# First edge loop of a four-layer graph network: the order of its turned one-hots, and the order of the work that prepares it

## The reference

```python
past, future = (edge_index[0], edge_index[1])
x_past = x[past]
x_future = x[future]
fwd_in = jnp.concatenate([x_future, x_past, edge_attr], axis=1)
flow_fwd = _mlp(fwd_in, W1f, b1f, W2f, b2f)
fwd_agg = jax.ops.segment_sum(flow_fwd, future, num_segments=x.shape[0])
bwd_in = jnp.concatenate([x_past, x_future, edge_attr], axis=1)
flow_bwd = _mlp(bwd_in, W1b, b1b, W2b, b2b)
bwd_agg = jax.ops.segment_sum(flow_bwd, past, num_segments=x.shape[0])
```

## Time and profile before

| | us |
|---|---|
| median of 3 runs | 2804.22 (2803.76 to 2804.41) |
| the profiled execution | 2801.62 |
| its span | 2799.8 |
| first table matmul starts (L893) | 819.76 |
| first and last `hidden` start (L926) | 862.4 and 1646.3 |

### The profile page before, as it was taken

One profiled execution on the slowest core, in us unless ns is written; L12 is line 12 of the kernel. 1 busy time (PEld: TensorE's weight loads), 2 busy tenths in 40 slices (PEclk: granted clock), 3 DMA queues, 4 the chain that ended last, 5 costly groups with the idle time before them and its releaser, 6 DMA issues. The chain is left out here.

```text
span 2799.8 us, 70675 instructions
## 1 busy us (share of the span) xinstructions
PE 2212.1 (79%) x26560; PEld 1628.7 (58%) x26560; DVE 1636.7 (58%) x4376; ACT 1368.2 (49%) x3156; POOL 1532.0 (55%) x1701
## 2 busy tenths in 40 slices
PE   0428787788727999999999967999999859995895
PEld 0103333333316888888888854666666559995773
DVE  5825444444405666666666656999999835552001
ACT  1005333333316888887888856888888600000110
POOL 2007777777756777777777734888888700000000
PEclk9967666656558999999999987999999969998997
DMA  8874444444330433343333425777777340007856
GB/s 352 363 288 112 113 113 114 113 114 113 109 89 16 163 120 118 118 157 125 117 118 118 163 102 153 199 192 200 199 192 200 94 83 3 3 3 313 334 228 288
DMA packets 252686, 427.70 MB, mean 153 GB/s; under 512 B 128564, under 2 KB 214222, under 8 KB 242725
## 3 DMA queue, kind: packets, MB, share of 16 engines
q1 hardware_dynamic: 194630, 337.86, 34.0%
q0 software_dynamic: 54800, 83.75, 12.3%
q10 hardware_dynamic: 2924, 1.57, 0.2%
HBM read 233.42 MB, written 209.72 MB: 158 GB/s over the span
## 5 line engine op out<-in xcount | busy, mean ns | idle before, releaser
L331 POOL DMA_INDIRECT sorted_edges<-s_records,s_index x400 | 476.3, 1191 | 311.5 <-issue 307.9
L803 POOL TENSOR_TENSOR e_ohw<-e_oh,e_rec 128x512 bf16<-128x512 bf16 x314 | 474.3, 1530 | 4.9 <-DVE e_oh L1056 4.9
L1524 PE MATMUL m_p_acc<-m_prod,m_oh 128*128 128x344 f32 x1250 | 400.6, 464 | 33.4 <-DVE m_prod L1585 22.6
L1524 PEld LDWEIGHTS m_p_acc<-m_prod,m_oh 128*128 128x128 f32 x1250 | 226.2, 191 | 148.1 <-issue 56.2
L1566 DVE TENSOR_TENSOR m_prod<-m_rec,m_coef 128x256 f32<-128x256 f32 x471 | 233.3, 546 | 0.0
L809 POOL TENSOR_TENSOR e_part<-e_rest,e_part 128x256 bf16<-128x256 f32 x157 | 104.0, 662 | 226.6 <-ACT e_part L871 226.6
L859 ACT ACTIVATE e_ohw<-e_oh,e_rec 128x128 bf16<-128x128 bf16 x628 | 216.2, 394 | 0.0
L1056 DVE TENSOR_TENSOR e_oh<-e_iota,e_rec 128x1024 bf16<-128x1024 f32 x157 | 212.2, 1353 | 0.2 <-DVE e_w_parts L91 0.2
L1782 PE MATMUL q_p_next<-q_g,pair 128*128 128x96 bf16 x4725 | 202.3, 207 | 0.0
L1782 PEld LDWEIGHTS q_p_next<-q_g,pair 128*128 128x128 bf16 x4725 | 201.3, 98 | 0.0
L1073 DVE COPY e_strip<-e_p_aw 128x512 f32<-128x512 f32 (+1 forms) x325 | 200.6, 660 | 0.0
(11 more groups left out here) (347 smaller groups left out, 4904.3 us busy)
## 6 DMA issues: line engine op xcount, KB each, us to landing
dense_strips<-e_strip SPq DMA_DIRECT2D x25, 3200.0 KB, 10.0
pair<-dense_strips SPq DMA_DIRECT2D x49, 1600.0 KB, 19.0
m_rec<-sorted_edges SPq DMA_DIRECT2D x138, 526.0 KB, 3.9
sorted_edges<-s_neg SPq DMA_DIRECT2D x5, 12560.0 KB, 68.5
pair<-dense_strips POOLq DMA_DIRECT2D x25, 800.0 KB, 8.9
e_rec<-sorted_edges SPq DMA_DIRECT2D x156, 108.0 KB, 2.3
sorted_edges<-s_records,s_index POOLq DMA_INDIRECT x400, 3.9
m_rec<-sorted_edges SPq DMA_DIRECT2D x12, 394.5 KB, 3.9
```

The lines of the kernel that those rows point to most:

```text
L331: pool.indirect_dma_start(dram["edges"], bass.IndirectOffsetOnAxis(ap=index[u % RING][:, c:c + 1], axis=0), record[u % RING][:, c, :], Non ...
L803: i = g_.tensor_tensor(ohw[g % 4][:, :, k, :], oh[s][:, :, 0, :], rec[s][:, :, c:c + 1].to_broadcast([P, G, P]), ALU.mult)
L1524: i = mm(p_acc[d % 2][:, 0:TERMS], oh[g % 4][:, t % G, :], prod[g % 3][:, t % G, :], start=(t % NB == 0), stop=(t % NB == NB - 1), skip_gr ...
```

## The change

1. In the loop, PE's `turn` is split into `turn_one_hots` and `turn_records`, both for group j+5, one-hots first. ACT's `copy_oh` stands ahead of `copy_rec`. SP's next load into a buffer of records waits for `rec_turned` in place of `turned`.
2. The 18 loads behind `d_b` are issued by SP, between the second and the third load of records, and no longer by ACT.
3. On DVE the fills and the `identb` cast stand ahead of the tables; `cut_weights`, with its wait for `d_b`, stands behind the fourth cut (i = 3); `one_hots(0)` to `one_hots(5)` follow the last six cuts, one each, and the loop makes only the later ones.

```diff
@@ sync @@
-                turned.before(sp, g, U)
+                rec_turned.before(sp, g, U)
...
             for g in range(2):
                 load(g)
+            sp.wait_ge(setup, 1)
+            for k, (wn, name) in enumerate(((1, "f"), (0, "b"))):
+                for i in range(6):
+                    sp.dma_start(w1e[16 * i:16 * i + 16, k, :], io["L0_gnn_W1" + name][2 * D:2 * D + 16, :]).then_inc(d_b, 16)
+                sp.dma_start(b1[k * H1:(k + 1) * H1, :], io["L0_gnn_b1" + name].unsqueeze(1)).then_inc(d_b, 16)
+                sp.dma_start(w2[k * H1:(k + 1) * H1, wn, :], io["L0_gnn_W2" + name]).then_inc(d_b, 16)
+                sp.dma_start(b2[:, :, wn, :], io["L0_gnn_b2" + name].unsqueeze(0).unsqueeze(0).to_broadcast([P, G, D])).then_inc(d_b, 16)
             for g in range(2, U):
                 load(g)
@@ scalar @@
-            act.wait_ge(setup, 1)
-            for k, (wn, name) in enumerate(((1, "f"), (0, "b"))):
-                for i in range(6):
-                    act.dma_start(w1e[16 * i:16 * i + 16, k, :], io["L0_gnn_W1" + name][2 * D:2 * D + 16, :]).then_inc(d_b, 16)
...
-                staged(j, (middle, 2), (copy_rec, 5), (copy_oh, 5), (weigh_first, 4), (relu1, 4), (weigh_last, 4), (relu2, 3))
+                staged(j, (middle, 2), (copy_oh, 5), (copy_rec, 5), (weigh_first, 4), (relu1, 4), (weigh_last, 4), (relu2, 3))
@@ tensor @@
-            def turn(g):
+            def turn_one_hots(g):
+                s = g % U
+                onehots.after(pe, g)
+                ohT_copied.before(pe, g, 1)
+                pe.sem_inc(prime, 1)
+                for k in range(2):
+                    for t in range(G):
+                        i = nc.tensor.transpose(p_oh[:, k, t, :], oh[s][:, t, k, :], identb[:, :])
+                turned.set_by(i)
+
+            def turn_records(g):
...
-                staged(j, (turn, 5), (hidden, 4), (second, 3), (sums, 1), (dense, 2))
+                staged(j, (turn_one_hots, 5), (turn_records, 5), (hidden, 4), (second, 3), (sums, 1), (dense, 2))
@@ vector @@
+            for i in range(TABLES):
+                n, to, y = table(i)
+                tab_hi.after(dve, i)
+                tab_low.before(dve, i, 2)
+                dve.sem_inc(prime, 1)
+                tab_cut.set_by(V.tensor_tensor(tab_rest[i % 2][:, 0:n, :], y, to[:, :, 0, :], ALU.subtract))
+                if i == 3:
+                    dve.wait_ge(d_b, 288)
+                    cut_weights(dve, V, w_chain, w1e[:, :, :].rearrange("p k h -> p (k h)"), w1_parts)
+                if i >= TABLES - READY:
+                    one_hots(i - (TABLES - READY))
+
+            def later_one_hots(g):
+                if g >= READY:
+                    one_hots(g)
...
-                staged(j, (copy_dense, 1), (copy_from, 0), (one_hots, 7), (add_bias, 3), (cut_rest, 3))
+                staged(j, (copy_dense, 1), (copy_from, 0), (later_one_hots, 7), (add_bias, 3), (cut_rest, 3))
```

More of the change, by code:

```diff
@@ L646, in layer0_edges_phase @@
         SETS, LATE = 3, 3
+        READY = 6
         x, tab, agg, ident, over = keep["x"], keep["tab"], keep["agg"], keep["ident"], keep["over"]
@@ L815, in _ @@
         def _(act):
-            act.wait_ge(setup, 1)
-            for k, (wn, name) in enumerate(((1, "f"), (0, "b"))):
-                for i in range(6):
-                    act.dma_start(w1e[16 * i:16 * i + 16, k, :], io["L0_gnn_W1" + name][2 * D:2 * D + 16, :]).then_inc(d_b, 16)
-                act.dma_start(b1[k * H1:(k + 1) * H1, :], io["L0_gnn_b1" + name].unsqueeze(1)).then_inc(d_b, 16)
-                act.dma_start(w2[k * H1:(k + 1) * H1, wn, :], io["L0_gnn_W2" + name]).then_inc(d_b, 16)
-                act.dma_start(b2[:, :, wn, :], io["L0_gnn_b2" + name].unsqueeze(0).unsqueeze(0).to_broadcast([P, G, D])).then_inc(d_b, 16)
             for i in range(TABLES + 1):
@@ L910, in turn @@
                 rec_turned.set_by(i)
-                onehots.after(pe, g)
-                ohT_copied.before(pe, g, 1)
-                pe.sem_inc(prime, 1)
-                for k in range(2):
-                    for t in range(G):
-                        i = nc.tensor.transpose(p_oh[:, k, t, :], oh[s][:, t, k, :], identb[:, :])
-                turned.set_by(i)
             def hidden(g):
@@ L1027, in _ @@
             V.memset(w2[:, :, :], 0.0).then_inc(setup, 1)
-            for i in range(TABLES):
-                n, to, y = table(i)
-                tab_hi.after(dve, i)
-                tab_low.before(dve, i, 2)
-                dve.sem_inc(prime, 1)
-                tab_cut.set_by(V.tensor_tensor(tab_rest[i % 2][:, 0:n, :], y, to[:, :, 0, :], ALU.subtract))
             for s in range(4):
@@ L1044, in _ @@
             V.tensor_copy(identb[:, :], ident[:, :]).then_inc(setup, 1)
-            dve.wait_ge(d_b, 288)
-            cut_weights(dve, V, w_chain, w1e[:, :, :].rearrange("p k h -> p (k h)"), w1_parts)
             dve.wait_ge(setup, 2)
```

## The result

The changed kernel takes 2842.75 us in the median of five runs (2830.89 to 2845.95), the kernel before 2804.41 us in its five (2803.76 to 2805.31). The ratio is 1.0121, with a 95% interval of 1.0105 to 1.0136: slower by 34 us by the ratio and 38 by the medians, where 56 us less were forecast. The profiled execution of the changed kernel is the shortest of the five, 2830.89 us with a span of 2829.1 us, so its trace shows 29 us of the loss against the span before of 2799.8 us.

What follows compares the result with a forecast made beforehand. A ring of dependences through `cut_rest`, PE, DVE and ACT was taken to set the loop's 5.025 us turn; 45 us net from the loop plus 11 from the preparation gave 2748 us, range 2726 to 2770.

Steps and rivals of the forecast that it cites:

- The ring, and what is late next: Loop: dependences from `cut_rest` to `cut_rest` set the turn; then ACT's `copy_rec` delays `second`; turn 5.025 to 4.72 us.
- Rival 1: Loop: ACT is no hindrance and the turn falls to 4.58 us; 2730 us in all, chance 0.25.
- rival 2: Loop: ACT's handover to `second` is slower by 0.15 to 0.2 us, turn 4.9 us; 2774 us, chance 0.12.
- rival 3: Loop: `copy_rec` becomes the whole ring and the turn grows, 5.15 us giving 2813 us; chance 0.04.
- The sign that was named: PE in the loop: a new gap of 0.1 to 0.2 us ahead of `second`, ended by ACT, would show the forecast bound.
- 156 equal turns: Loop: the saving of one turn, 5.025 to 4.72 us, times 156 wins 47.6 us.
- The wait ahead of `second`: PE in the loop: `second` now waits for ACT's `copy_rec`, leaving 0.1 to 0.2 us idle a turn.
- What would make it wrong is a ring through POOL or DVE: Loop: only an unseen ring through POOL or DVE, each with over 1 us a turn free, would upset the whole forecast.
- `copy_from`'s turns: DVE in 25 turns of the loop: the bias waits for nothing, DVE is 0.11 us late, 2.6 us lost.
- The preparation: Before the loop: ACT casts early, `d_b` is complete at 832 (829 to 841); 11 us won, ends 7 and 14.
- One-hots between the tables: DVE in the preparation: one-hots take 1.25 to 2.07 us beside POOL, so a table takes 1.94 to 2.76 us.
- The sum's lower end: Whole kernel: 48 us from the loop and 14 from the preparation give 2742 us or so.

Runs made afterwards that it cites:

- e4: The kernel before with each strip write cut into five of 640 KB, one issued in each turn: 2802.24 us, ratio 1.0006.
- e3: The changed kernel with each strip write cut into five of 640 KB, one issued in each turn: 2766.63 us, ratio 0.9886.
- e13: e9 with a copy of 128x1152 elements on ACT ahead of `copy_rec`, so that `second` must wait for it: 2925.59 us, ratio 1.0449.
- e14: The changed kernel with PE's `second` placed behind `sums`, so that it needn't wait for `copy_rec`: 2812.21 us, ratio 1.0041.
- e9: The changed kernel with ACT copying records ahead of one-hots again, PE still turning one-hots first: 2772.38 us, ratio 0.9889.
- e12: e3 with the weights cut behind the ninth table, not the fourth, and copies to `w1s` issued ahead of SP's wait for `x`: 2760.47 us, ratio 0.9848.
- e11: The changed kernel with PE's and ACT's old orders restored, the turning still written in two steps: 2797.34 us, ratio 0.9985.

## Why the prediction was wrong, point by point

- **The ring, and what is late next: right.** The idle time ahead of the records' loads is gone, `copy_rec` became what `second` waits for, and the quiet turn is 4.68 us (forecast 4.72, bounds 4.67 to 4.77). Rival 1 (ring 4.58) and rival 2 (turn 4.9) don't hold; rival 3's condition, `copy_rec` as the whole ring, isn't met. The sign that was named, a new gap of 0.1 to 0.2 us ahead of `second`, is smaller: PE's loads stand idle for 0.07 us there (1253.08 + 0.87 = 1253.95, then 1254.02), and `second` starts 1.65 us behind `hidden`'s load, where it was 1.53 before.
- **156 equal turns: the step that failed.** The sum took one turn from the timeline times 156 and forecast 47.6 us. Once in a node block a turn holds a strip write, and these writes had been harmless in the kernel before (e4: splitting them there brings nothing). In the new order 17 of the 25 stop PE for 2 to 5 us, and 13 of these stops leave it at half the clock for 3.4 or 6.8 us. That cost 85 us against 731, and turned a gain into 32 us lost. With the writes in parts the same loop gives back most of the forecast: e3 takes 751 us for it, 33 less than before; the other 15 us go with the short stops that it has left.
- **The wait ahead of `second`: its price was put at its own length.** The prediction counted the new wait as 0.1 to 0.2 us of idle time, and it is about 0.1. Its real price is that PE then comes out of the strip writes without instructions. e13 and e14 tie the stops to this wait, the reserve of 3 to 4 us in place of 6 to 7 says how, and q8's packets and the count of 256 show that it is the supply of instructions.
- **"What would make it wrong is a ring through POOL or DVE": missed.** Neither is it. The thing unseen was no dependence in the program, but PE's supply of instructions, which comes over the DMA engines too, and these are 0.35 busy in the mean and full for 10 us at a time. No rival had the strip writes in it, so the range of 2726 to 2770 couldn't hold the time.
- **`copy_from`'s turns: condition right, price too high.** In the changed kernel they can't be told apart from the stops, but in e3 they can. There the bias in such a turn waits for nothing, as forecast, and comes 1513.51 - 1508.76 = 4.75 us behind the last; the next follows in 1518.15 - 1513.51 = 4.64. Two usual turns make 9.36, so 0.03 us is lost each time and under 1 us in all, not 2.6.
- **SP's wait for `rec_turned`:** no cost, as said. e9 and e3 have it and gain.
- **The preparation: mechanism right, term mis-sized.** ACT's first cast was early as forecast (823.2 in a stage that began 2.2 us late). `d_b` was taken at 832, within 829 to 841; it was complete at 840.4 (838.2 on the clock of the kernel before, whose stage began 2.2 us earlier), since the last 64 KB load took 10.9 us to land and not 3.3 to 8.6. The 11 us forecast became 5.1 counted from the stage's first issue. e12, with that wait moved out of the way, wins 12.2.
- **One-hots between the tables:** 1.57 to 1.94 us beside POOL's 1.64 to 1.78 (1.15 when alone), inside the bounds of 1.25 to 2.07. The rule that the prediction cites from the Trainium skill ("GPSIMD Engine Reference", Key points) agrees in kind: every one-hots between the tables met POOL's part and was slow, and so was POOL. But with a whole step of 2.09 us a table (850.13 - 848.04) it was nearer to the short bound of 1.94 than to 2.76.
- **The sum's lower end:** 2742 takes 48 us for the loop, the middle of the forecast; its own bound of 4.67 us a turn gives 55 less 3, and 2738. The range of 2726 to 2770 held both, and the measured time lies 73 us above it.

## What to carry to other kernels

Before a turn of a loop is multiplied by its count, look for what happens only in some turns, above all large DMA writes, and ask what shares the engines with them: the instruction queue does. A transfer that fills the DMA engines for 10 us is safe only as long as PE's reserve of instructions lasts, and an edit that touches neither can shorten that; parts spread over the turns cost nothing here (e4) and gave back 73 us (e3). A wait of 0.1 us can decide it. When an idle time "<-issue" stands in the middle of a run of matmuls, look at the packets of kind "instruction" around it, count the engine's instructions from one such stop to the next (multiples of 256 here), and look at the granted clock behind it.

## What the runs showed of the hardware

- PE can run out of instructions in straight code. A write of 3200 KB fills the DMA engines for 10 us, the next q8 packet starts 5 to 11 us behind it, and PE stands still for 2 to 5 us.
- One q8 packet of 16 KB brings 256 of PE's instructions, and all 104 stops counted in 13 traces stand at the same place in a block of 256. PE goes on 2.2 to 2.7 us behind the packet's start.
- Five writes issued at once still bring stops of up to 3.8 us (1.0047 against 1.0121 for one); of five or ten spread over the turns only stops of up to 1.6 us are left.
- 13 of 17 stops of 1.8 to 4.7 us were followed by 3.4 or 6.8 us at a granted clock of 0.50, four by none.
- A semaphore wait on PE at `second`, of about 0.1 us in the changed kernel, decides whether the long stops come, and whether the packets' instructions are there 3 to 4 us or 6 to 7 us ahead of their use. A wait of about 0.5 us at the turning of the records, as before and in e11 and e14, doesn't bring them. Turns of 4.81 us without the former (e9) have hardly any, turns of 5.51 us with it (e13) have them.

**What stays open.** Why this wait halves the reserve wasn't found, nor why a longer one at the turning of the records doesn't. q8's packets show when a block arrives, not when it was asked for: in e9 two packets lie 13.1 us apart around the write at 962.9 us and PE runs on, in the changed kernel 12.1 us apart around the one at 939.9 and it stops for 2.9. Nor was it found what keeps a packet out for 5 us and more, beyond that the engines are full then. Whether a wait at another place in the matmuls, such as ahead of `sums` or `dense`, would do the same wasn't tried.
